# State recurrence of a two-layer block: four states in flight, SBUF operations over 1024 columns, and one accumulating transfer a state

## The chip, the cores and the metric

The kernel runs on one core of a Trainium2 chip. The metric is the device time of one execution in microseconds. Three runs of the kernel before gave 6723.36, 6741.94 and 6750.02 us; their median, 6741.94 us, is the time that the change is compared with.

## What is computed

The input is 16 sequences of 512 tokens with 256 features, in float32. Each sequence goes through two layers. Layer 0 is an attention whose scores are squared (q times k over 16 features a head, 16 heads, squared and made causal, then divided by their sum) and a gated product with int8 weights. Layer 1 is a state recurrence in both directions and a gated product whose operands are rounded to fp4 in blocks of 16. The recurrence sets the shape of the kernel. Per direction, with 512 channels `d` and 16 states `n`:

```python
dt = softplus(einsum('blr,dr->bld', dtr, Wdt) + bdt)
A  = -exp(Alog)
def step(h, ins):
    dt_t, u_t, B_t, C_t = ins
    h = exp(dt_t[..., None] * A) * h + (dt_t * u_t)[..., None] * B_t[:, None, :]
    y_t = einsum('bdn,bn->bd', h, C_t)
    return (h, y_t)
```

So for each of 32 pairs of direction and state the kernel scans 512 channels over 512 tokens and adds C times the result to a running sum y.

## The kernel before

**Slots.** Each engine runs a program of 128 slots per sequence (`SLOTS`), one slot for each group of 128 channels (`m`, four of them) of each of the 32 states. `one(b)` of each engine walks the slots. In each slot it issues its share of the recurrence and then its list of side work (`side`, L432) from a table, `PLAN`, that the `row(...)` calls from L284 on write out by hand: piece, direction, how many sequences ahead, and for each engine the slots of its items; a fraction orders items inside a slot. Five queues work through their own lists in order and meet only through semaphores. Side work of up to four neighbouring sequences lies in the slots of one: attention of sequence b+1, fp4 product of b-1, and so on. `sequences` (L441) runs b from -2 to 16, so that b = -2 and -1 fill the pipeline and the last ones drain it.

**The recurrence, by engine.** POOL multiplies B and dt*u into a state buffer (`inflow`, L723), three slots ahead of the scan. ScalarE (ACT) writes exp(dt*A) into one of three PSUM banks (`decay`, L943), two slots ahead. VectorE (DVE) scans in place (`scan`, L1214). When the four groups of a state are scanned, TensorE (PE) turns them, one block of 128 tokens per slot, into one of two PSUM banks (`turn_state`, L1497), four slots behind. Of the four token blocks of a state, DVE weighs two with C and adds them to `yT` in one operation (`add_state`, L1225). ACT weighs the other two into `hc` (`weigh_last`, L951), and POOL adds `hc` to `yT` (`add_last`, L734). Three state buffers `hb` (`HBS`) limit how far POOL can run ahead: `inflow` of state s waits until state s-3 has been turned.

**Side work of note.** Attention: `score` (L1307) makes products over 64 partitions, one head at a time; ACT squares them (`square`, L815), POOL masks them (`causal_mask`, L669), `weigh` (L1322) multiplies by v in column groups of 32 and `attn_divide` (L1081) ends a group of four heads. One of the three PSUM side banks (`SUMS`) is kept for the sums of `weigh` through slots 14 to 52 (`HELD`). The softplus of the step sizes takes four ACT operations, two DVE operations (L1178, L1180) and three POOL operations (L704, L707, L709) per group. `quantise` and `quantise_tail` round to fp4.

**Setup.** Before the slots, PE turns all weights, DVE rounds the fp4 weights (L991 to L1008), ACT and DVE evict the turned blocks, and SP stores them to DRAM; every engine waits until all 13 stores have landed. SP reloads weights into shared buffers later, in slots of the `l_` rows. SP also broadcasts one row of B per state into one of two halves of `bS` (`spread_b`, L636).

## Time and profile before

| | before |
|---|---|
| median of 3 runs | 6741.94 us |
| profiled execution, its own time | 6731.3 us |
| its span, first to last instruction | 6729.6 us |
| PE busy | 5027.9 us (75%) |
| POOL busy | 4928.8 us (73%) |
| DVE busy | 4791.3 us (71%) |
| ACT busy | 4129.1 us (61%) |
| granted TensorE clock, mean | 0.829 |

The profile is of one execution. Busy time is the time in which an engine has an instruction running; "idle before" is the time in which it had none just before the named instruction, with what ended the wait. The transfers took 14.4% of the time of the 16 DMA engines.

### The profile page before, as it was taken

What the parts mean: (1) busy time and instruction counts of PE and PEld (TensorE: products, weight loads), DVE (VectorE), ACT (ScalarE), POOL (GpSimd) and SP (SyncE); (2) the same over time, 40 slices, a digit from 0 to 9 for tenths busy, and PEclk for the clock granted to TensorE, in tenths of its full rate; (3) what the DMA queues carried; (4) which work ended last, traced back from release to release, by engine and by line L of the source; (5) the groups of instructions that cost most, each with busy time, mean ns of one, the idle gap of its engine ahead of it and who ended that gap; (6) DMA issues with size and microseconds to landing.
All of it is one profiled execution on the core that took longest, in us unless ns stands there. A gap on an engine that the chain in (4) does not pass through costs nothing.

```text
span 6729.6 us, 82733 instructions
## 1 busy us (share of the span) xinstructions
PE 5027.9 (75%) x21900; PEld 3136.3 (47%) x21900; DVE 4791.3 (71%) x6116; ACT 4129.1 (61%) x6696; POOL 4928.8 (73%) x3914
## 2 busy tenths in 40 slices
PE   3787777778778777877768777777877777787666
PEld 2344444454445444454444545444444544545444
DVE  3157777676877778687676867767687776868774
ACT  1366666666666666666666666666666666666563
POOL 0077777777777877778777777878777777777785
PEclk6678888888888888888888888888888888888777
DMA  3011111111111111111111111111111111111110
GB/s 111 15 43 38 51 45 47 38 47 45 50 51 47 45 42 45 46 51 50 40 50 40 50 45 48 45 38 53 40 50 51 47 47 38 45 46 48 37 46 26
DMA packets 152792, 308.76 MB, mean 46 GB/s; under 512 B 20870, under 2 KB 58310, under 8 KB 149926
## 3 DMA queue, kind: packets, MB, share of 16 engines
q1 hardware_dynamic: 152278, 302.80, 14.4%
q8 instruction: 214, 3.51, 0.2%
q14 instruction: 300, 2.46, 0.1%
HBM read 285.90 MB, written 16.84 MB: 45 GB/s over the span
## 4 chain that ended last, share of the span: by engine, by line
PE 47%; DVE 17%; issue 13%; POOL 11%; ACT 10%; DMA 1%; DVEq 0%; SPq 0%; POOLq 0%; ACTq 0%
PE psum L1497 8%; PE psum L1307 8%; POOL arena_m L723 5%; DVE arena_m L1214 4%; PE psum L1351 4%; PE psum L1422 3%; PE psum L1477 3%; PE psum L1430 3%; DVE arena_m L1164 3%; POOL arena_m L734 3%; PE psum L1385 3%; PE psum L1367 2%; PE psum L1439 2%; DVE arena_m L1225 2%; PE psum L1413 2%
## 5 line engine op out<-in xcount | busy, mean ns | idle before, releaser
L723 POOL TENSOR_TENSOR arena_m<-bS,arena_m 128x512 f32<-128x512 f32 x2048 | 2621.8, 1297 | 305.6 <-PE psum L1497 231.3
L1214 DVE TENSOR_TENSOR_SCAN arena_m<-psum,arena_m 128x512 f32<-128x512 f32 x2048 | 2448.0, 1209 | 322.4 <-POOL arena_m L723 193.6
L1497 PE MATMUL psum<-ident,arena_m 128*128 128x128 f32 x8192 | 1437.2, 312 | 540.1 <-DVE arena_m L1225 289.2
L734 POOL TENSOR_TENSOR arena_m<-arena_m,hc 128x512 f32<-128x512 f32 x1024 | 1307.3, 1277 | 569.0 <-ACT hc L951 345.7
L943 ACT ACTIVATE psum<-arena_m,Aneg 128x512 f32<-128x512 f32 x2048 | 1396.1, 690 | 428.2 <-DVE arena_m L1214 382.9
L1497 PEld LDWEIGHTS psum<-ident,arena_m 128*128 128x128 f32 x8192 | 1103.8, 160 | 1180.5 <-issue 535.6
L1225 DVE SCALAR_TENSOR_TENSOR arena_m<-psum,Ct,arena_m 128x512 f32<-128x512 f32 x1024 | 747.3, 730 | 379.8 <-PE psum L1497 375.0
L1307 PE MATMUL psum<-arena_a 64*128 64x512 f32 (+3 forms) x2048 | 829.2, 528 | 205.3 <-ACT arena_a L815 79.4
L951 ACT ACTIVATE hc<-psum,Ct 128x512 f32<-128x512 f32 x1024 | 696.3, 680 | 375.3 <-PE psum L1497 300.7
L815 ACT ACTIVATE arena_a<-psum 128x384 f32<-128x384 f32 (+1 forms) x768 | 401.8, 525 | 452.9 <-PE psum L1307 425.5
L1307 PEld LDWEIGHTS psum<-arena_a 64*128 64x128 f32 x2048 | 369.6, 208 | 541.3 <-issue 231.9
L1385 PE MATMUL psum<-wB,arena_m 128*128 128x352 f32 x1024 | 430.3, 553 | 84.2 <-DVE arena_m L1164 46.9
L669 POOL TENSOR_SCALAR_AFFINE_SELECT arena_a<-arena_a 128x512 f32<-128x512 f32 (+1 forms) x192 | 157.9, 822 | 394.4 <-ACT arena_a L815 394.3
L1164 DVE SCALAR_TENSOR_TENSOR arena_m<-psum,convw,arena_m 128x509 f32<-128x509 f32 (+2 forms) x384 | 286.7, 747 | 142.3 <-ACT arena_m L876 132.9
L1351 PE MATMUL psum<-arena_a,wA 128*128 128x512 bf16 x1152 | 323.2, 433 | 81.9 <-issue 55.4
L1422 PE MATMUL psum<-xnT,wU 128*128 128x512 f32 x512 | 289.7, 695 | 44.4 <-DVE arena_m L1164 43.5
L678 POOL TENSOR_TENSOR arena_a<-arena_a 128x704 f32<-128x704 f32 (+1 forms) x80 | 145.0, 1813 | 216.8 <-DVE arena_a L1002 216.8
L1385 PEld LDWEIGHTS psum<-wB,arena_m 128*128 128x128 f32 x1024 | 216.6, 234 | 178.2 <-issue 88.4
L1404 PE MATMUL psum<-ident,arena_a 128*128 128x128 f32 (+1 forms) x384 | 86.7, 360 | 275.9 <-POOL arena_a L684 217.4
L1430 PE MATMUL psum<-xnT,wZ 128*128 128x512 f32 x512 | 261.3, 642 | 0.5 <-ACT arena_m L918 0.5
L704 POOL TENSOR_TENSOR arena_m<-arena_m 128x512 f32<-128x512 f32 x128 | 170.7, 1333 | 104.4 <-ACT arena_m L903 104.3
L1477 PE MATMUL psum<-wO,arena_m 128*128 128x256 f32 x1024 | 237.2, 383 | 1.9 <-issue 0.8
(151 smaller groups left out, 7216.9 us busy)
## 6 DMA issues: line engine op xcount, KB each, us to landing
bS<-brow SPq DMA_DIRECT2D x512, 256.0 KB, 3.2
wB<-kept_B SPq DMA_DIRECT2D x16, 1408.0 KB, 6.2
wU<-kept_U SPq DMA_DIRECT2D x32, 512.0 KB, 4.5
wZ<-kept_Z SPq DMA_DIRECT2D x32, 512.0 KB, 4.6
wO<-kept_O SPq DMA_DIRECT2D x32, 512.0 KB, 4.8
wA<-kept_A SPq DMA_DIRECT2D x16, 768.0 KB, 5.6
wB<-kept_B SPq DMA_DIRECT2D x16, 768.0 KB, 4.3
wA<-kept_A SPq DMA_DIRECT2D x16, 640.0 KB, 4.2
```

The costliest lines, as they stand in the source:

```text
L723: pool.tensor_tensor(hb[s % HBS][:, m, :], bS[:, s % 2, :], du[r][:, m, :], ALU.mult).then_inc(m_dbu.sem, 1)
L734: pool.tensor_tensor(yT[:, 2 + i, :], yT[:, 2 + i, :], hc[:, i, :], ALU.add).then_inc(m_yl.sem, 1)
L943: act.activation(EB[j % EBS], dt[r][:, m, :], ACT.Exp, scale=Aneg[:, r, m, n:n + 1]).then_inc(m_dA.sem, 1)
L951: act.activation(hc[:, i, :], HT[1], ACT.Copy, scale=Ct[:, r, 2 + i, n:n + 1]).then_inc(m_hc.sem, 1)
L1164: dve.scalar_tensor_tensor(u[:, m, late:T], src[:, 0:T - late], convw[:, r, m, tap:tap + 1], u[:, m, late:T], ALU.mult, ALU.add).then_inc( ...
L1214: dve.tensor_tensor_scan(v, EB[j % EBS], v, 0.0, ALU.mult, ALU.add).then_inc(m_scan.sem, 1)
L1225: dve.scalar_tensor_tensor(yT[:, i, :], HT[0], Ct[:, r, i, n:n + 1], yT[:, i, :], ALU.mult, ALU.add).then_inc(m_y.sem, 1)
L1307: ins = pe.matmul(bank("a_score", None, w)[:, c:c + n], kT[rows, ht, i * P:(i + 1) * P], qm[rows, j, i * P:T], start=True, stop=True)
L1351: ins = pe.matmul(bank(piece, None, m), w[:, k, m * P:(m + 1) * P], xparts[:, c, k, :], start=(k == 0 and c == 0), stop=(k == KD - 1 and c ...
L1385: ins = pe.matmul(bank(piece, None, w)[:, 0:FIH], xTq[:, k, i * P:(i + 1) * P], w_[:, k, c * FIH:(c + 1) * FIH], start=(k == 0), stop=(k = ...
L1422: ins = pe.matmul(bank("p_in", r, m), wU[:, k, m * P:(m + 1) * P], xnT[:, k, :], start=(k == 0), stop=(k == KD - 1))
L1497: ins = pe.transpose(HT[pos % 2][:, m * P:(m + 1) * P], hb[s % HBS][:, m, i * P:(i + 1) * P], ident[:, :])
```

## The change

The change has six parts.

1. Recurrence. There are four state buffers in place of three (`HBS`). `inflow` becomes one POOL operation on 128x1024 for two channel groups, every second slot, four slots ahead. `turn_state` runs six slots behind the scan in place of four (`TURN`). It turns the token blocks in the order 0, 1, 2, 3; DVE adds blocks 0 and 1, ACT weighs blocks 2 and 3.
2. `add_last` is no POOL operation any more but one DMA transfer per state, issued by POOL: `hc` (now 4 KB a partition for each of two states) is added to `yT[:, 2:4, :]`, 512 KB. It waits for both blocks of `hc` and for the transfer of the state before.
3. Attention. `score` issues the products of two heads, one on partitions 0 to 63 and one on 64 to 127, in turn. `weigh` runs once per group of four heads and takes any free side bank, which is held until the division. `asq` is laid out in four parts; `square` has one more operation for every third item, the mask is 16 operations of 128x512, and the division is two operations.
4. Softplus. The correction takes one DVE operation in place of two and one more ACT operation.
5. Setup. The fp4 weights are not rounded before the slots but in slots 12 to 17 of b = -1, turned in slots 36 to 49, stored from slot 56; the waits for the stores move to slot 92 of b = -1, SP's wait for the first ten stays in slot 0 of it.
6. Space and plan. `wZ` shares its buffer with `wU`, `wX` with `wO`; their loads wait for each other's readers. All rows of `PLAN` are new.

The diff, cut to its core:

```diff
-    HBS = 3
+    HBS = 4
-    ORDER = (0, 2, 1, 3)
+    TURN = 6
-        wZ = sb("wZ", [P, KD, DI])
-        wX = sb("wX", [P, NM, P])
+        wZ = wU
+        wX = wO[:, 0:NM // 2, :].rearrange("p m (h c) -> p (m h) c", h=D // P)
-        hc = sb("hc", [P, 2, DI])
+        hc = sb("hc", [P, 2, 2, DI])
...
-        row("d_turn", 1, -1, PE=[4, 4.2, 4.3, 6.1])
+        row("d_turn", 1, -1, PE=[3, 3, 7, 7])
...
-        row("p_in", 1, 0, PE=[13, 16, 19.1, 22], ACT=[14, 16, 19, 22])
+        row("p_in", 1, 0, PE=[14, 16, 18, 21], ACT=[14, 17, 19, 22])
...
+        row("l_X", 1, 0, SP=[8])
+        row("d_out", 1, -1, PE=[9, 10, 11, 11.1], DVE=[10, 12])
...
+        FRONT, FP4_IN, FP4_DVE, FP4_PE, FP4_OUT, FREE = 0, 2, 12, 36, 56, 92
...
@@ gpsimd @@
                 if m == 0:
-                    before = s - HBS if s >= HBS else min(s - 2, -1)
-                    pool.wait_ge(*m_hT.by(b, NT * (before + 1)))
+                    pool.wait_ge(*m_hT.by(b, NT * (s - HBS + 1)))
...
-                pool.tensor_tensor(hb[s % HBS][:, m, :], bS[:, s % 2, :], du[r][:, m, :], ALU.mult).then_inc(m_dbu.sem, 1)
+                two = slice(m, m + 2)
+                pool.tensor_tensor(hb[s % HBS][:, two, :], bS[:, s % 2, :].unsqueeze(1).to_broadcast([P, 2, T]), du[r][:, two, :],
+                                   ALU.mult).then_inc(m_dbu.sem, 1)
...
+            def add_last(b, s):
                 r, n = divmod(s, NS)
-                pool.wait_ge(*m_hc.by(b, c + 1))
+                pool.wait_ge(*m_hc.by(b, 2 * s + 2))
                 if n == 0:
-                    pool.wait_ge(*m_y0.by(b, NT * r + 2 + i + 1))
+                    pool.wait_ge(*m_y0.by(b, NT * (r + 1)))
                 else:
-                    pool.wait_ge(*m_yl.by(b, c - 1))
-                pool.tensor_tensor(yT[:, 2 + i, :], yT[:, 2 + i, :], hc[:, i, :], ALU.add).then_inc(m_yl.sem, 1)
+                    pool.wait_ge(*m_yl.by(b, 16 * s))
+                apart(pool)
+                pool.dma_start(yT[:, 2:4, :], hc[:, s % 2, :, :], accum_op=ALU.add).then_inc(m_yl.sem, 16)
...
-                    ab, ja = spot(b, j + 3)
-                    if exists(ab):
+                    ab, ja = spot(b, j + 4)
+                    if ja % 2 == 0 and exists(ab):
                         inflow(ab, ja)
-                    if j % 2:
-                        lb, jl = spot(b, j - 7)
-                        if exists(lb):
-                            add_last(lb, jl // 2)
+                    lb, jl = spot(b, j - TURN - 3)
+                    if jl % NT == NT - 1 and exists(lb):
+                        add_last(lb, jl // NT)
...
@@ scalar @@
-                act.activation(src, src, ACT.Exp, scale=-1.0).then_inc(m_ex.sem, 1)
+                act.activation(cx[:, c, :], src, ACT.Exp, scale=-1.0).then_inc(m_ex.sem, 1)
...
-                act.activation(lx[:, c, :], src, ACT.Ln, bias=1.0).then_inc(m_ln.sem, 1)
+                act.activation(src, cx[:, c, :], ACT.Identity, bias=1.0).then_inc(m_w.sem, 1)
+                act.wait_ge(*m_w.by(b, q + 1))
+                act.activation(lx[:, c, :], src, ACT.Ln).then_inc(m_ln.sem, 1)
...
-                act.wait_ge(*m_yl.by(b, c - 1))
-                act.activation(hc[:, i, :], HT[1], ACT.Copy, scale=Ct[:, r, 2 + i, n:n + 1]).then_inc(m_hc.sem, 1)
+                act.wait_ge(*m_yl.by(b, 16 * (s - 1)))
+                act.activation(hc[:, s % 2, i, :], HT[i], ACT.Copy, scale=Ct[:, r, 2 + i, n:n + 1]).then_inc(m_hc.sem, 1)
...
+                    wb, jw = spot(b, j - TURN - 2)
+                    if jw % NT >= 2 and exists(wb):
+                        weigh_last(wb, 2 * (jw // NT) + jw % NT - 2)
...
@@ vector @@
-                dve.tensor_scalar(cx[:, c, :], src, 1.0, -1.0, ALU.add, ALU.add).then_inc(m_c1.sem, 1)
-                dve.wait_ge(*m_c1.by(b, q + 1))
-                dve.tensor_tensor(cx[:, c, :], src, cx[:, c, :], ALU.subtract).then_inc(m_c2.sem, 1)
+                dve.scalar_tensor_tensor(cx[:, c, :], bank("p_dt", r, m), 1.0, cx[:, c, :], ALU.subtract,
+                                         ALU.subtract).then_inc(m_c2.sem, 1)
...
+                    if first(b) and FP4_DVE <= j < FP4_DVE + 6:
+                        fp4_weights(j - FP4_DVE)
...
+                    yb, jy = spot(b, j - TURN - 1)
+                    if jy % NT < 2 and exists(yb):
+                        add_state(yb, 2 * (jy // NT) + jy % NT)
...
@@ tensor @@
+                if w % 2 == 0:
+                    apart(pe)
+                    return
                 for i, c in UNITS[un]:
                     n = T - i * P
-                    ins = pe.matmul(bank("a_score", None, w)[:, c:c + n], kT[rows, ht, i * P:(i + 1) * P], qm[rows, j, i * P:T],
-                                    start=True, stop=True)
-                ins.then_inc(a_s_ps.sem, 1)
+                    for half in range(2):
+                        rows = slice(64 * half, 64 * half + 64)
+                        ins = pe.matmul(bank("a_score", None, w - 1 + half)[:, c:c + n], kT[rows, ht, i * P:(i + 1) * P],
+                                        qm[rows, j, i * P:T], start=True, stop=True)
...
-                    pe.wait_ge(*m_yl.by(b, 2 * (NS * (r + 1) - 1) + i - 1))
+                    pe.wait_ge(*m_yl.by(b, 16 * NS * (r + 1)))
...
-                if pos % 2 == 0:
-                    pe.wait_ge(*m_y.by(b, c // 2))
+                if i < 2:
+                    pe.wait_ge(*m_hc.by(b, 2 * s - 1 + i))
                 else:
-                    pe.wait_ge(*m_hc.by(b, c // 2))
+                    pe.wait_ge(*m_y.by(b, 2 * s - 1 + i))
```

## Rows read from the trace of the kernel before

**Rows 1.** The page, busy time by engine and its slices.

```profile
PE 5027.9 (75%) x21900; PEld 3136.3 (47%) x21900; DVE 4791.3 (71%) x6116; ACT 4129.1 (61%) x6696; POOL 4928.8 (73%) x3914
```

**Rows 2.** All scans (L1214): duration, first and last start, who waits.

```profile
L1214 DVE TENSOR_TENSOR_SCAN arena_m<-psum,arena_m x2048: 1158/1211/1226, 367.8 to 6619.8; 128x512 f32<-128x512 f32 x187
```

**Rows 3.** One sequence by stage: stretch, busy (x instructions) of PE, PEld, DVE, ACT, POOL, clock, DMA.

```profile
3117.00:3138.00 21.00, 14.60 (x80) 12.54 (x81) 14.33 (x16) 9.50 (x15) 18.47 (x16) 0.76 0.22 64
3138.00:3262.00 124.00, 107.20 (x454) 55.22 (x451) 83.53 (x102) 81.00 (x142) 91.15 (x78) 0.88 0.13 39
3262.00:3302.00 40.00, 26.43 (x136) 17.52 (x136) 32.65 (x43) 28.24 (x46) 38.11 (x32) 0.78 0.17 51
3302.00:3400.00 98.00, 77.10 (x377) 54.17 (x378) 79.88 (x105) 63.99 (x97) 69.79 (x51) 0.90 0.17 55
3400.00:3516.00 116.00, 81.09 (x322) 51.80 (x321) 85.94 (x114) 73.93 (x120) 92.08 (x71) 0.84 0.14 41
```

**Rows 4.** Groups of POOL, same sequence: count, busy us, mean ns, idle before it.

```profile
L723 POOL TENSOR_TENSOR arena_m<-bS,arena_m 128x512 f32<-128x512 f32 x129 | 165.3, 1299 | 19.8 <-PE psum L1497 14.6 <-DMA bS<-brow 5.2
L734 POOL TENSOR_TENSOR arena_m<-arena_m,hc 128x512 f32<-128x512 f32 x65 | 83.0, 1277 | 35.5 <-ACT hc L951 21.3 <-ACT arena_m L913 13.9
...
L697 POOL TENSOR_TENSOR xL<-xA,arena_a 128x1024 f32<-128x1024 f32 x1 | 2.4, 2350 | 4.7 <-ACT arena_a L782 4.7
```

**Rows 5.** DMA issues by line: KB each, median us from issue to landing.

```profile
bS<-brow SPq DMA_DIRECT2D x512, 256.0 KB, 3.2
wB<-kept_B SPq DMA_DIRECT2D x16, 1408.0 KB, 6.2
wU<-kept_U SPq DMA_DIRECT2D x32, 512.0 KB, 4.5
...
wO<-kept_O SPq DMA_DIRECT2D x32, 512.0 KB, 4.8
...
out<-xF SPq DMA_DIRECT2D x16, 512.0 KB, 3.0
```

**Rows 6.** Products of score (L1307) and weigh (L1322), same sequence, columns of rows 3.

```profile
3117.00:3516.00 399.00, 50.00 (x128) 22.09 (x128) 0.85 0.15 46
...
3117.00:3516.00 399.00, 11.10 (x128) 2.98 (x128) 0.85 0.15 46
```

**Rows 7.** PE in order of time: start, us; weigh in four column groups, then score.

```profile
3213.48 0.86 PE L1322 MATMUL psum<-arena_a,vx 128*32 128x256 f32 x16
...
3216.92 0.91 PE L1307 MATMUL psum<-arena_a 64*128 64x384 f32 x2
```

**Rows 8.** Groups of DVE and of ACT, same sequence.

```profile
L1178 DVE TENSOR_SCALAR arena_m<-psum 128x512 f32<-128x512 f32 x8 | 5.5, 682 | 9.2 <-ACT arena_m L903 9.2
...
L903 ACT ACTIVATE arena_m<-psum 128x512 f32<-128x512 f32 x8 | 4.8, 598 | 0.6
```

**Rows 9.** Setup in order of time: Aneg on ACT, first fp4 step, PE resumes, PE in slots.

```profile
36.29 0.31 ACT L753 ACTIVATE Aneg<-arena_m 128x128 f32<-128x128 f32 x1 [34.19 <-DMA arena_m<-in_L_attn_b_Alog]
...
31.82 1.22 DVE L991 TENSOR_REDUCE hc<-arena_m 88x64 f32<-88x1024 f32 x1 [8.11 <-DMA arena_m<-in_L_ffn_w_down]
...
79.63 4.89 PE L1252 MATMUL psum<-ident,arena_m 128*128 128x128 f32 x28 [59.84 <-DVE arena_m L1030]
...
122.65 1.94 PE L1263 MATMUL psum<-ident,arena_a 128*128 128x128 f32 x8 [30.46 <-ACT arena_a L782]
```

**Rows 10.** Two stretches of the fill, columns of rows 3.

```profile
122.00:250.00 128.00, 112.94 (x336) 54.95 (x336) 7.96 (x25) 38.35 (x73) 9.84 (x12) 0.59 0.03 10
250.00:366.00 116.00, 70.40 (x208) 35.94 (x209) 35.56 (x73) 47.54 (x73) 29.25 (x23) 0.76 0.12 34
```

**Rows 11.** Waits in the same sequence: total us, times, longest.

```profile
DVE arena_m L1225 <- PE psum L1497: 23.0, 10, 4.8
POOL arena_m L734 <- ACT hc L951: 21.3, 9, 6.2
...
POOL arena_m L734 <- ACT arena_m L913: 13.9, 2, 8.8
```

More of the change, by code:

```diff
@@ new lines, in block_kernel @@
+        row("f_rest", None, 1, DVE=[63, 64, 66, 66])
+        row("f_gate", None, 1, PE=[65, 65, 67, 67, 68.2, 70], ACT=[68, 68, 69, 69, 70.1, 72.1])
+        row("q_quant", None, -1, DVE=[66, 67, 67, 69, 70, 71], POOL=[78, 78, 80])
+        row("d_turn", 0, 0, PE=[68, 68.1, 73, 74])
+        row("i_turn", 1, 0, PE=[69, 71, 75.1, 75.2], ACT=[70, 72, 77, 78])
+        row("f_silu", None, 1, ACT=[69, 74])
+        row("d_gate", 0, 0, DVE=[69, 69, 74, 74.2])
+        row("f_up", None, 1, PE=[71, 72, 74, 75, 76, 77.1], DVE=[73, 74.1, 75, 76, 77, 78])
@@ new lines, in block_kernel @@
+        row("d_out", 0, 0, PE=[77, 78, 80, 80], DVE=[78, 83])
+        row("f_down", None, 1, PE=[78, 80, 82, 82], DVE=[81, 84])
+        row("z_in", 1, 0, PE=[81, 84, 86, 86], ACT=[82, 86.1, 86.2, 89])
+        row("m_stat2", None, 1, ACT=[86], DVE=[81, 85, 85])
+        row("q_turn", None, -1, PE=[83, 83], ACT=[84, 85])
+        row("m_norm2", None, 1, ACT=[88], DVE=[86])
+        row("m_x", None, 1, POOL=[88])
+        row("q_gate", None, -1, PE=[89, 90, 94, 96, 101.1, 102, 106.1, 108], ACT=[90, 91, 95.1, 97.1, 103, 103, 108, 108])
@@ L390, in block_kernel @@
         }
-        HELD = range(14, 53)
+        divided = [j for j in range(SLOTS) for q in PLAN["DVE"][j] if q[0] == "a_sums"]
+        held = {}
         jobs_of = [[], [], []]
@@ L1030, in _, with fp4_weights @@
                 dve.tensor_copy(dst, src).then_inc(setup_dve.sem, 1)
-            dve.wait_ge(setup_act.sem, NJ // 2)
-            dve.wait_ge(a_neg.sem, 2)
-            dve.wait_ge(stored.sem, 16 * (STORES + 1))
+            for n in range(0, NJ, 2):
+                evict(n)
+            def fp4_weights(part):
+                s, c = divmod(part, 2)
+                rows, cols = (GP, 8 * D) if s < 2 else (P, KD * FI)
+                half = cols // 2
+                dve.wait_ge(loaded["fp4"].sem, 16 * 3)
+                if part:
+                    dve.wait_ge(wquant.sem, QOPS * part)
+                for k in range(QOPS):
+                    quantise(s_fp4[s][0:rows, c * half:(c + 1) * half], wtmp[0:rows, 0:half], w_am, w_sc, w_inv, 0, wquant,
+                             QOPS * part, k)
             def norm_stat(n, b, src, k):
```

430 lines of the change are left out of this document (220 added, 210 removed).

## The prediction

> **What bounds the kernel now.** I read the page first. No engine is full: PE 75%, POOL 73%, DVE 71%, ACT 61% of the span [rows 1]. So the limit is not one engine but the five in-order queues that follow one another within a few slots; in each stage the busiest one sets the pace and the others wait for it.
>
> The second view is the line of the scans, one per slot. There are 2048 from 367.8 to 6619.8 us [rows 2], 6252 us; over 2047 intervals that is 3.054 us a slot, 391 us a sequence; with full side work it is 399 us, as in the sequence of [rows 3]. Before the first scan lie 368 us of setup and fill, behind the last 109 us of drain. The first sequences lack some side work, so I take 397 us for a full one and count the stretch as 6252 / 397 = 15.75 sequences.
>
> The third view cuts one sequence into five stages [rows 3]. The reader is to see that the bound moves:
> - 3117 to 3138 (slots 0 to 7, the change of direction): POOL 18.5 of 21 us.
> - 3138 to 3262 (8 to 47, attention): PE 107.2 of 124 us, 86%; POOL 91.2, DVE 83.5, ACT 81.0.
> - 3262 to 3302 (48 to 63): POOL 38.1 of 40 us, 95%; DVE 32.7.
> - 3302 to 3400 (64 to 95): DVE 79.9 and PE 77.1 of 98 us; nobody is full.
> - 3400 to 3516 (96 to 127, fp4 and the next softplus): POOL 92.1 of 116, DVE 85.9, PE 81.1.
>
> The fourth view, the waits, shows the lockstep: in this sequence DVE's add waits 23.0 us for turned blocks, and POOL's add 21.3 us for ACT's `hc` and 13.9 us for the first terms [rows 11].
>
> **The change part by part.** Against the profiled execution (6731.3 us), per sequence unless said otherwise.
>
> (a) POOL loses 64 adds of 1277 ns, 82 us [rows 4]. A pair of inflows costs 2 x 1299 = 2.60 us now; one operation on 128x1024 took 2.35 us [rows 4], so 64 of them save 0.25 x 64 = 16 us. It gains 32 DMA issues. No row shows POOL issuing a DMA. I bound one issue by nothing (all beside other work) and by the two adds that it replaces, 2.55 us, and take 1.3 us, one POOL operation on 512 columns: 42 us. The net is about -56 us, between -98 and -16.
>
> (b) The transfer. 512 KB were stored in 3.0 us and loaded in 4.5 and 4.8 us; 1408 KB took 6.2 us [rows 5], so 896 KB more cost 1.7 us. An accumulate must also read its destination. Counted as 1024 KB it lands in 4.5 + 512 / 896 x 1.7 = 5.5 us. The ends are 3.0 us and two full loads, 9.6 us. POOL waits for the transfer of the state before, in its queue, and behind that wait stand the next inflow, the softplus sums and fp4 tails; DVE's scan waits for the inflow. So the distance of two issues, 5.5 + 1.3 = 6.8 us, is a floor for a state. A state takes 12.2 us in the mean (four slots), but not evenly. Of the 511 distances from each fourth scan of [rows 2] to the next, 104 are under 8 us. With every distance shortened by 7%, the floor adds about 60 us in the run at 6.8 us, 181 us at 8 us and 435 us at 10 us. I take 60 us.
>
> By the Trainium skill, page DMA: Bandwidth & Descriptors, section Anatomy of one DMA, a transfer issued by GpSimd takes about 2.0 us and its bytes over 436 GB/s. As an estimate from that page, with 1 MB, that is 4.4 us and the 60 us would be near 5. No row here shows a transfer of this kind.
>
> At each change of direction PE's `d_turn` of blocks 2 and 3 waits for the last transfer; it is issued in POOL's slot 8, while `d_turn` stands in PE's slot 7. Before, it waited for one 1.3 us add. That is up to 5.5 us, twice a sequence, in stages where PE works 14.6 of 21 us. I charge the first stage its whole gain (3 us) and nothing more.
>
> (c) Attention. The scores hold PE for 50.0 us in 128 instructions [rows 6]. They use 64 partitions. The trace has no pair on both halves, but it has the other split: 16 weigh products in four column groups took 0.86 us, less than two score products of 384 columns, 0.91 us [rows 7]. So groups do overlap on this PE, and I take half, -22 us (ends 0 and -25). What is late next in the attention stage: PE 85, DVE 83.5 less 32 corrections and a few, 81, ACT 81 + 4 us (part d), POOL 91 less 25. At 80% for the busiest, the stage takes 85 / 0.8 = 106 us in place of 124: 18 us. All three side banks serve the scores between the holds, which works the same way; I don't count it apart.
>
> By the Trainium skill, page TensorEngine Tiling (Array Packing), section PSUM Bottleneck, tiling speeds up PE but not the evacuation of PSUM. If that ruled here, ACT's squares would be late next and the 18 us would shrink to nearly nothing, which is the second rival's result.
>
> (d) Softplus: DVE loses 8 x 682 ns = 5.5 us, ACT gains one operation like L903, 8 x 598 ns = 4.8 us [rows 8], and 16 short squares. ACT is the least busy of the four, so I cost its part at nothing; without that cover it is 9 us.
>
> (e) The other stages. Slots 48 to 63: POOL falls from 38.1 to about 28, DVE at 32.7 in 0.9 of the time gives 36 us: 4 us. Slots 64 to 95: no bound is removed, but the turn has three slots of room behind the scan in place of one, and the inflow four in place of three: 3 us. Slots 96 to 127: POOL falls from 92 to about 77, and DVE's 86 at 79% give 109 us: 6 us, as POOL's three-operation softplus chain stays. Slots 0 to 7: nothing. The sum is 18 + 4 + 3 + 6 = 31 us; I take 3 off for SP, whose queue now stands at `l_X` in slot 8 until PE's `d_out` of slot 11, with the next B rows behind it. 28 us a sequence, 28 x 15.75 = 441 us.
>
> (f) Setup. The fp4 rounding starts at 31.8 us and PE resumes at 79.6 us behind it [rows 9]: 48 us. Then come the stores and their landing, and PE turns the first attention block at 122.7 us [rows 9]. Without the rounding ACT's evictions still wait for `Aneg`, 36.3 us [rows 9]; 13 of them by 0.6 us end at 44, and with some 7 us for the first norm the same turn comes at about 54 us. That is 68 us. The rounding moves beside the fill's attention, where DVE works 8.0 of 128 us while PE works 112.9 [rows 10]; it is hidden but for the divisions behind it, and without this cover it costs its 48 us. I charge 15 us for it and the 18 moved turns. The score pairs take about 20 us off the same stage. The drain gets two slots longer and a transfer, 6 us. Net -67 us.
>
> **The sum.** 6731.3 - 441 + 60 - 67 = 6283 us in the profiled execution. The median of the runs is 10.6 us above that execution's time, so the median after is 6294, rounded to 6290 us.
>
> **The rivals.**
>
> 1. The accumulating transfer is the bound (slower). It is one chain of 512 transfers, each waiting for the one before. Its price is set by the distance L of two issues. With all other gains, the run takes 6681 us at L = 10, 6876 at 11, 7121 at 12 and 7444 at 13; it decides from L = 10.3 us. For it: no transfer inside SBUF, issued by POOL or adding is in the trace, and 10.3 is only 0.7 above my upper end of 9.6 plus no issue time. Against it: 512 KB land in 3.0 to 4.8 us [rows 5] and the DMA engines are used to 0.14 to 0.22 [rows 3]. Its time: 7120 us.
>
> 2. The score pairs don't overlap, or ACT's squares take PE's place. Then the attention stage gives 2 in place of 18 us: 16 x 15.75 = 252 us dearer, 6540 us. For it: ACT works 81 of 124 us there, and scores wait for banks. Against it: the column groups overlap [rows 7].
>
> 3. The lockstep stays. PE's turn of block 0 now waits in the slot in which ACT weighs block 2 of the state before, where there was a slot between them; what the longer distances give is lost there. POOL's gain is hidden, only setup counts: 6742 - 67 + 30 = 6705 us. For it: no engine was above 86% over 124 us. Against it: two stages have an engine at 86 and 95%.
>
> 4. Looser queues give more. With the busiest engine at 90% in the middle stages a sequence takes 340 us: 57 x 15.75 = 898 us off, 5840 us with (b) and (f). For it: there are more buffers in every loop but the two PSUM banks. Against it: DVE reaches such shares only in stretches.
>
> **How the numbers follow.** Forecast 0.48 (6120 to 6450, most of it from the landing time); rival 2 0.15; rival 3 0.12; rival 4 0.08; rival 1 0.17. Half a per cent (34 us) is about what a measurement tells from no change. Rival 3 lies on that edge; a bit over half of it counts as the same: same 0.07. Faster 0.48 + 0.15 + 0.05 + 0.08 = 0.76. Slower 0.17. The range, 5990 to 6750 us, leaves out half of rival 4 and rival 1 nearly whole, 0.2.
>
> **What would show each step.** POOL busy near 4000 us, with a gap or an issue of 1 to 2 us at each transfer; landings of 5 to 6 us in the list of DMA issues. The score line at 25 to 30 us a sequence. The scans' stretch at 5870 us, the first one at about 300 us. In the stages, PE and DVE near 80% in slots 8 to 47. I am wrong on the sign if POOL's longest wait in total is for its own transfers and states come at equal distances; wrong on (c) if two score products in a pair start one after another.

## The result and the profile after

The changed kernel takes 6798.6 us (6791.6 to 6807.8), the kernel before in the same runs 6743.3 us (6723.4 to 6750.0): ratio 1.0088, 95% interval 1.0063 to 1.0113. It is slower by 0.9%, where 6290 us was predicted, with a range of 5990 to 6750 us. The mean granted TensorE clock is 0.828, against 0.829 before, so the clock is not what differs.

Every piece of work that was to go did go. The page of the changed kernel: busy time by engine, the DMA queue of POOL (packets, MB, share of the 16 DMA engines), groups of instructions (busy us, mean ns, idle before) and the issue of the transfer with its landing in us; beside [rows 1], [rows 4] and [rows 5]:

```profile
span 6793.3 us, 80279 instructions
PE 4619.7 (68%) x21853; PEld 2952.4 (43%) x21900; DVE 4730.9 (70%) x6052; ACT 4209.5 (62%) x7080; POOL 3926.6 (58%) x2442
...
q0 software_dynamic: 73728, 268.47, 21.1%
...
L762 POOL TENSOR_TENSOR arena_m<-bS,arena_m 128x1024 f32<-128x1024 f32 x1024 | 2547.7, 2537 | 983.0 <-PE psum L1565 509.7
...
L774 POOL DMA_DIRECT2D arena_m<-hc x512 | 468.5, 915 | 684.6 <-ACT hc L999 491.0
...
L1378 PE MATMUL psum<-arena_a 64*128 64x512 f32 (+3 forms) x2048 | 443.4, 535 | 160.6 <-ACT arena_a L860 66.8
...
arena_m<-hc POOLq DMA_DIRECT2D x512, 512.0 KB, 4.6
```

POOL has 1002 us less work, PE 408 us, the transfer is issued in 0.9 us, has landed after 4.6 us and takes up 21% of the DMA engines. And yet the scans, with the first and last start beside [rows 2], take longer:

```profile
L1268 DVE TENSOR_TENSOR_SCAN arena_m<-psum,arena_m x2048: 1157/1214/1225, 289.8 to 6669.0; 128x512 f32<-128x512 f32 x187
```

The first scan comes 78 us earlier, the stretch from first to last is 6379 us in place of 6252, the drain 124 in place of 110. So all of the loss lies in the stretch from the first scan to the last. One sequence by stage, in the columns of [rows 3] and cut at the same slots (0 to 7, 8 to 47, 48 to 63, 64 to 95, 96 to 127):

```profile
3094.00:3107.00 13.00, 8.83 (x48) 7.41 (x48) 12.43 (x14) 8.33 (x14) 9.58 (x6) 0.71 0.45 93
3107.00:3247.00 140.00, 91.30 (x475) 51.03 (x476) 88.37 (x105) 84.34 (x160) 71.37 (x52) 0.85 0.31 72
3247.00:3288.00 41.00, 26.84 (x159) 18.69 (x157) 29.30 (x44) 30.23 (x50) 30.86 (x20) 0.82 0.41 96
3288.00:3387.00 99.00, 72.11 (x352) 49.58 (x356) 77.95 (x105) 62.45 (x95) 54.14 (x29) 0.87 0.43 110
3387.00:3498.00 111.00, 82.99 (x327) 53.58 (x326) 81.68 (x110) 76.66 (x124) 79.35 (x49) 0.84 0.34 81
```

The attention stage, where PE was to fall from 107 to 85 us and the stage from 124 to 106, has PE at 91 and lasts 140 us: its busiest engine is at 65%. (Most of that loss lies in the first eight of these slots; see the table below.) The stage of slots 48 to 63 lost 7 us of POOL's work and takes 41 us where it took 40. What is there instead are waits. The list of the changed kernel (total us, times, longest):

```profile
DVE arena_m L1279 <- PE psum L1565: 791.4, 415, 8.7
PE psum L1565 <- ACT hc L999: 748.7, 448, 7.3
...
POOL arena_m L762 <- PE psum L1565: 509.7, 151, 9.6
...
POOL arena_m L774 <- ACT hc L999: 491.0, 125, 12.0
POOL arena_m L762 <- DMA bS<-brow: 473.1, 61, 18.4
...
PE psum L1537 <- DMA arena_m<-hc: 79.4, 16, 9.3
```

The same list for the queue of SP alone:

```profile
SPq L658 <- ACT xd L936: 945.1, 31, 48.0
SPq L589 <- PE psum L1546: 832.9, 30, 33.0
...
SPq L646 <- POOL xL L736: 264.0, 15, 53.4
```

The same waits of the kernel before, in the same columns: PE's turn for ACT's `hc`, and POOL's inflow for the broadcast B rows.

```profile
PE psum L1497 <- ACT hc L951: 122.0, 121, 4.6
...
POOL arena_m L723 <- DMA bS<-brow: 74.3, 15, 5.8
```

Three suspects stand in these lists: PE's turn waits for ACT's weighing (the new order 0, 1, 2, 3), POOL waits for B rows that SP fetches (the SP queue stands at `keep_rows`, L658, and at `l_X`, L589), and `d_turn` (L1537) waits for the transfer. A list of waits doesn't say what a wait costs, so each was tried in a kernel of its own.

### The profile page after: what moved, and what is told of

Read it like the earlier page. It is cut to its first block and busy times, and to the rows that moved or that the text cites. A ratio compares the mean times of both kernels' runs of the same rounds, so it can differ in the third digit from the quotient of the medians.

```text
span 6793.3 us, 80279 instructions
## 1 busy us (share of the span) xinstructions
PE 4619.7 (68%) x21853; PEld 2952.4 (43%) x21900; DVE 4730.9 (70%) x6052; ACT 4209.5 (62%) x7080; POOL 3926.6 (58%) x2442
## 3 DMA queue, kind: packets, MB, share of 16 engines
q1 hardware_dynamic: 152278, 302.80, 14.1%
## 5 line engine op out<-in xcount | busy, mean ns | idle before, releaser
L762 POOL TENSOR_TENSOR arena_m<-bS,arena_m 128x1024 f32<-128x1024 f32 x1024 | 2547.7, 2537 | 983.0 <-PE psum L1565 509.7
L1268 DVE TENSOR_TENSOR_SCAN arena_m<-psum,arena_m 128x512 f32<-128x512 f32 x2048 | 2443.1, 1210 | 201.5 <-ACT psum L991 167.8
L774 POOL DMA_DIRECT2D arena_m<-hc x512 | 468.5, 915 | 684.6 <-ACT hc L999 491.0
L860 ACT ACTIVATE arena_a<-psum 128x512 f32<-128x512 f32 (+3 forms) x1024 | 381.4, 444 | 523.6 <-PE psum L1378 342.1
L708 POOL TENSOR_SCALAR_AFFINE_SELECT arena_a<-arena_a 128x512 f32<-128x512 f32 x256 | 193.8, 814 | 669.1 <-ACT arena_a L860 668.9
L1378 PE MATMUL psum<-arena_a 64*128 64x512 f32 (+3 forms) x2048 | 443.4, 535 | 160.6 <-ACT arena_a L860 66.8
L1454 PE MATMUL psum<-wB,arena_a 128*128 128x352 f32 x1024 | 412.1, 541 | 62.2 <-DVE arena_m L1222 60.3
L1328 PE MATMUL psum<-ident,arena_a 128*128 128x128 f32 x640 | 128.9, 361 | 331.4 <-ACT arena_a L825 282.2
L1378 PEld LDWEIGHTS psum<-arena_a 64*128 64x128 f32 x2048 | 195.1, 216 | 312.6 <-issue 178.0
L1491 PE MATMUL psum<-xnT,wU 128*128 128x512 f32 x512 | 267.5, 649 | 32.2 <-DVE arena_m L1222 29.7
L1454 PEld LDWEIGHTS psum<-wB,arena_a 128*128 128x128 f32 x1024 | 210.4, 223 | 162.0 <-issue 55.1
L1499 PE MATMUL psum<-xnT,wU 128*128 128x512 f32 x512 | 257.1, 638 | 4.5 <-DVE xA L1172 4.2
```

Of the source, the lines that this page charges most:

```text
L762: pool.tensor_tensor(hb[s % HBS][:, two, :], bS[:, s % 2, :].unsqueeze(1).to_broadcast([P, 2, T]), du[r][:, two, :], ALU.mult).then_inc(m_ ...
L774: pool.dma_start(yT[:, 2:4, :], hc[:, s % 2, :, :], accum_op=ALU.add).then_inc(m_yl.sem, 16)
L860: act.activation(asq[i][:, 2 * (j % 2) + j // 2, :], bank("a_score", None, w)[:, c:c + n], ACT.Square).then_inc(a_sq.sem, 1)
L1268: dve.tensor_tensor_scan(v, EB[j % EBS], v, 0.0, ALU.mult, ALU.add).then_inc(m_scan.sem, 1)
L1378: ins = pe.matmul(bank("a_score", None, w - 1 + half)[:, c:c + n], kT[rows, ht, i * P:(i + 1) * P], qm[rows, j, i * P:T], start=True, stop ...
L1454: ins = pe.matmul(bank(piece, None, w)[:, 0:FIH], xTq[:, k, i * P:(i + 1) * P], w_[:, k, c * FIH:(c + 1) * FIH], start=(k == 0), stop=(k = ...
```

## The experiments

b-kernels edit the kernel before, e-kernels the changed one. Where a kernel also needs small moves of side work, its expectation says so. Kernels are compared by their medians; the 95% intervals of the ratios are about 0.2% (some 12 us) to either side. The table is worked out from the starts of the scans (mean over sequences 3 to 14 of the 16, us for each range of slots; the column in brackets is a part of the one before it) and is used throughout:

```
kernel        first scan  sequence   0-7   8-31  (8-15)  32-47  48-63  64-95  96-127
before            367.8     397.9   21.3   63.8  (13.5)   59.3   40.1   99.3   114.2
after             289.8     406.2   13.6   76.5  (27.6)   63.4   40.8  101.1   110.8
b1_dma            368.8     408.8   27.8   65.1  (13.4)   61.0   39.4  104.4   111.1
b2_order          350.9     447.7   28.0   82.3  (16.2)   68.7   42.6  106.4   119.7
e2_sp_rows        295.1     397.3   13.5   76.4  (27.7)   58.6   39.2   99.0   110.5
e3_pool_add       293.8     407.6   13.6   74.7  (25.2)   60.0   44.3  102.4   112.6
e1_alternate      296.3     402.5   13.9   77.9  (32.1)   59.1   42.0  102.7   106.9
e5_alt_sp         297.9     392.2   14.0   78.6  (32.5)   51.2   42.8   99.0   106.7
e10_change        296.2     388.0   14.0   72.2  (27.4)   54.4   41.5   98.9   106.9
e14 (one half)    306.8     420.3   13.5   87.8  (31.2)   66.5   40.0  101.6   110.8
```

The table shows where the changed kernel loses its 8.3 us a sequence. Slots 0 to 7 get 7.7 us shorter and slots 8 to 15 get 14.1 us longer: with the turn six slots behind the scan, the end of the direction before (`d_turn`, gate, `d_out`) stands in later slots, partly behind slot 7. Slots 0 to 15 together go from 34.8 to 41.2 us. Slots 16 to 47, the rest of the attention, take 112.3 us where they took 109.6, although PE's work there fell from 93.6 to 70.3 us.

**The transfer alone, and the order alone, in the kernel before.**

b1_dma:

```diff
-                pool.tensor_tensor(yT[:, 2 + i, :], yT[:, 2 + i, :], hc[:, i, :], ALU.add).then_inc(m_yl.sem, 1)
+                pool.dma_start(yT[:, 2:4, :], hc[:, s % 2, :, :], accum_op=ALU.add).then_inc(m_yl.sem, 16)
```

> The kernel before with the accumulating transfer alone: one transfer a state in place of two POOL additions, hc for two states, space made by letting the fp4 product's input share a buffer with the attention's; order, distances and side work as before. Theory C: slower than before, 6800 us or more. Theories A and B: faster, by 1 to 4%, 6470 to 6680 us, since POOL's 1307 us of additions become 470 us of issues and nothing else is touched.

Measured: 6857.6 us, ratio 1.019 (1.0173 to 1.0208). The transfer makes the kernel before slower by 122 us, as theory C had it. (The shared buffer of the fp4 input, which makes the space, was not tried apart.) Its page and its waits:

```profile
PE 5041.7 (74%) x21838; PEld 3158.7 (46%) x21900; DVE 4818.1 (70%) x6116; ACT 4123.4 (60%) x6696; POOL 4068.0 (59%) x3402
...
L723 POOL TENSOR_TENSOR arena_m<-bS,arena_m 128x512 f32<-128x512 f32 x2048 | 2723.5, 1488 | 960.7 <-PE psum L1497 795.9
```

```profile
PE psum L1468 <- DMA arena_m<-hc: 129.8, 17, 8.7
```

POOL lost 861 us and waits 796 us for PE's turns in their place (231 before). In slots 48 to 63, where POOL had been 95% busy [rows 3], its work fell from 38.0 to 30.3 us and the stage only from 40.1 to 39.4 us: POOL's work alone did not set it. 6.5 of the 10.9 us lost a sequence lie in slots 0 to 7, where `d_turn` now waits for a landing.

b2_order puts the new turning order into the kernel before at its distance of four slots:

```diff
-                i = ORDER[pos]
-                if pos % 2 == 0:
-                    pe.wait_ge(*m_y.by(b, c // 2))
+                if i < 2:
+                    pe.wait_ge(*m_hc.by(b, 2 * s - 1 + i))
```

> The kernel before with one part of the change alone: token blocks turned in the order 0, 1, 2, 3, DVE adding the first two and ACT weighing the last two, all distances and side work as before. Theory A (the order costs the time: PE's turn now waits for ACT's weighing in the same slot, 748.7 us in the changed kernel against 122.0): slower than before by 2 to 6%, about 6880 to 7150 us, with PE's wait for the hc line at 30 us a sequence or more. Theory B (SP's queue stands at its own waits and the B rows come late) and theory C (the accumulating transfer costs it): within 0.7% of before, 6700 to 6790 us.

Measured: 7447.0 us, ratio 1.1056 (1.1038 to 1.1075), the largest effect of all the runs: theory A in kind, but far above its 2 to 6%.

```profile
DVE arena_m L1222 <- PE psum L1492: 868.8, 461, 6.3
PE psum L1492 <- ACT hc L949: 843.3, 489, 5.6
```

The turn of block 0 and ACT's weighing of block 2 of the state before now stand in one slot and wait for one another in turn; DVE's add stands behind. It costs in every range of slots, most in the attention.

**What the order costs at greater distances.** `TURN` is the distance of the turn behind the scan, six in the changed kernel.

e7_turn5 sets `TURN = 5` in the changed kernel. e6_alt5 sets it too and restores the old order (its core):

```diff
-    TURN = 6
+    TURN = 5
+    ORDER = (0, 2, 1, 3)
```

> Control for the one before: the changed kernel with the turn five slots behind the scan, in the changed kernel's own order. Both theories: 6750 to 6900 us; if it is faster than 6700 us, the distance and not the order explains a gain of the one before.

> The changed kernel with the old order of the token blocks (0, 2, 1, 3; DVE and ACT take turns, one PSUM bank each) and the turn five slots behind the scan in place of six; every row of side work as in the changed kernel. Theory A (the order is what eats the gain): 6200 to 6550 us, and PE's wait for the hc line falls from 748.7 us below 250 us. Rival (the long wait for hc is only PE's slack, since PE is 68% busy here): within 1% of the changed kernel, 6730 to 6870 us.

Measured: e7_turn5 7136.6 us (ratio 1.0605), e6_alt5 6761.1 us (1.0046). Both times miss what was expected. e7_turn5 lies above its range: the sixth slot alone is worth 338 us in the new order. e6_alt5 lies in the rival's range, although PE's wait for `hc` fell to 219 us as theory A had it; only beside e7_turn5 does it show that at distance five the order costs 376 us.

e1_alternate has the old order at distance six; `d_turn` of the first direction, one pair of scores and one softplus row are moved by a slot.

> The changed kernel (6799 us) with the turning order of before, 0, 2, 1, 3, at its own distance of six slots: PE's turn and ACT's weighing of one state lie in different slots again. A first-stage d_turn, one pair of scores and one softplus row are shifted by one slot, since at this order and distance the queues would otherwise wait in a circle. It computes the same. Theory (the order is a cost that the distance of six hides only in part): at a distance of five the order was worth 7137 - 6761 = 376 us, so here some of it remains; PE's wait for ACT's hc falls from 749 to under 300 us in total and the time lies at 6600 to 6720 us. Rival (at six slots the order costs nothing more, what is left comes from the SP queue and the side plan): 6780 to 6820 us, with the wait gone but the same time lost elsewhere.

Measured: 6717.2 us (6703.1 to 6727.5), ratio 0.9977 (0.9968 to 0.9987), 1.2% under the changed kernel.

```profile
POOL arena_m L763 <- PE psum L1567: 720.5, 139, 13.8
...
POOL arena_m L763 <- DMA bS<-brow: 460.0, 61, 21.7
...
PE psum L1567 <- ACT hc L1000: 347.1, 164, 6.6
```

The wait for `hc` fell by 402 us and the time by only 81; POOL's wait for the turns grew from 510 to 721 us in its place. So the order costs 712 us at distance four, 376 at five, 81 at six. The first of these is from the kernel before, which differs in more than the distance, and the last includes the moved side work: slots 8 to 15 got 4.5 us longer here, slots 16 to 47 7.4 us shorter. The time lies at the upper end of the theory's range, but the wait didn't fall under 300.

**The SP queue.** e2_sp_rows moves six rows of the changed kernel's SP plan behind what they wait for:

```diff
-        row("p_rows", 1, 0, SP=[26])
-        row("l_X", 1, 0, SP=[8])
-        row("l_X", 0, 1, SP=[78])
-        row("l_x", None, 2, SP=[86])
+        row("p_rows", 1, 0, SP=[42])
+        row("l_X", 1, 0, SP=[12])
+        row("l_X", 0, 1, SP=[86])
+        row("l_x", None, 2, SP=[92])
```

(and `l_g1` from 82 to 84, `store` from 119 to 122).

> The changed kernel with six rows of SP's list moved to later slots, behind what they wait for (p_rows from 26 to 42, l_X from 8 to 12 and from 78 to 86, l_g1 82 to 84, l_x 86 to 92, store 119 to 122). Theory B: POOL's wait for the B rows (473 us) falls below 120 us and with it the time, to 6400 to 6550 us. Theory A: that wait falls, but PE's and DVE's waits grow in its place; 6700 to 6800 us. Theory C: no change, 6750 to 6800 us.

Measured: 6648.1 us (6647.6 to 6651.0), ratio 0.9874 (0.9857 to 0.989), 2.2% under the changed kernel and already faster than before. The wait for the B rows fell below 120 us as theory B had it; the time stayed above its 6400 to 6550 us. Its waits:

```profile
PE psum L1565 <- ACT hc L999: 799.0, 438, 7.4
...
POOL arena_m L762 <- DMA bS<-brow: 105.8, 15, 7.4
```

```profile
SPq L658 <- ACT xd L936: 267.1, 16, 32.6
```

`keep_rows` had been moved by the change from slot 42 to 26, while ACT writes `xd` in slot 32 of its plan; `l_X` had gone from 14 to 8 and `l_x` from 102 to 86. SP stood there, the B rows behind it were not fetched, POOL's inflow stood without them, and DVE's scan without the inflow. With the row back at 42, slots 32 to 47 fall from 63.4 to 58.6 us; 1.6 us more come in slots 48 to 63 and 2.1 in 64 to 95. The six rows were moved together, so what each is worth is read only from where the slots got shorter. The wait for `hc` grew in the same run by 50 us, and the time fell all the same.

**The two causes together, and the change of direction.** e5_alt_sp has the old order at distance six and the SP rows moved:

> The kernel of the run before this one (order 0, 2, 1, 3, distance six) with the six rows of the SP queue moved as in e2_sp_rows. It computes the same. Theory (order and SP queue are two separate costs): 150 us below e1_alternate, and below e2_sp_rows (6648 us) by what e1_alternate lies below the changed kernel, so 6450 to 6600 us. Rival (both were ways of waiting for one bound that lies under both, such as DVE's and POOL's own work in the stages): 6620 to 6670 us, the same as e2_sp_rows.

Measured: 6555.7 us (6552.6 to 6561.9), ratio 0.9741 (0.9724 to 0.9757). The order gives 92 us here and 81 without the SP rows, the SP rows 161 and 151: at distance six these are two costs that add up. e8_alt5_sp, the same at distance five:

> Old order, turn five slots behind, and the six rows of SP's list behind what they wait for. If the two causes are separate, the time falls by the gain of the old order and by the 150 us of SP's rows: 6050 to 6400 us. If they share the same stall, it is that of the old order alone.

Measured: 6678.1 us, ratio 0.9931, far above the expected 6050 to 6400. At distance five the SP rows are worth only 83 us (6761.1 against 6678.1), so the two costs don't add up there. The sixth slot is worth 122 us, and 44 without the SP rows moved.

In both the changed kernel and e5_alt_sp one place stands out. The changed kernel in order of time at the first change of direction, first PE, then DVE (start, us, in brackets the idle time before and its releaser):

```profile
3106.14 0.63 PE L1565 MATMUL psum<-ident,arena_m 128*128 128x128 f32 x4
3111.28 1.96 PE L1537 MATMUL psum<-ident,arena_m 128*128 128x128 f32 x8 [4.51 <-DMA arena_m<-hc]
...
3117.81 1.89 PE L1546 MATMUL psum<-wO,arena_m 128*128 128x256 f32 x8
```

```profile
3113.89 1.21 DVE L1268 TENSOR_TENSOR_SCAN arena_m<-psum,arena_m 128x512 f32<-128x512 f32 x1
3122.00 0.69 DVE L1251 TENSOR_TENSOR xF<-psum,xM 128x512 f32<-128x512 f32 x1 [6.89 <-PE psum L1546]
3122.61 1.21 DVE L1268 TENSOR_TENSOR_SCAN arena_m<-psum,arena_m 128x512 f32<-128x512 f32 x1
```

`d_turn` stands in PE's slot 7, the transfer that it needs is issued in POOL's slot 8. PE idles 4.5 us, and then turn, gate and `d_out` follow in a chain while no scan runs: 8.7 us between two scans. e10_change moves the chain behind the transfer:

```diff
-        row("d_turn", 1, -1, PE=[3, 5, 7, 7])
-        row("d_gate", 1, -1, DVE=[6, 6, 9, 9])
-        row("d_out", 1, -1, PE=[9, 10, 11, 11.1], DVE=[10, 12])
-        row("l_X", 1, 0, SP=[12])
+        row("d_turn", 1, -1, PE=[3, 5, 9, 9])
+        row("d_gate", 1, -1, DVE=[6, 6, 10, 10])
+        row("d_out", 1, -1, PE=[11, 11, 12, 12.1], DVE=[12, 13])
+        row("l_X", 1, 0, SP=[15])
```

> e5_alt_sp (6556 us) with the turn of blocks 2 and 3 at the first change of direction moved from PE's slot 7 to slot 9, behind the transfer that it waits for, the gate that follows from DVE's slot 9 to 10, the first d_out from 9 and 10 to 11, and one row of the SP queue (l_X) from 12 to 15, as it waits for d_out. It computes the same. In e5_alt_sp the scans of slots 9 and 10 take 18.7 us of the 388.6 us of a sequence: PE stands 4.1 us for the transfer, then turn, gate, d_out and correction follow one another with the other engines idle (DVE 9.4 us for d_out, POOL 22 us for the squares behind it). Theory (the period is made of such waits of a queue's head; with the turn behind the transfer they go): slots 8 to 15 fall from 32.5 to under 27 us, the run by 60 to 120 us, 6440 to 6500 us. Rival (the chain only moves, two slots later): 6540 to 6570 us.

Measured: 6485.0 us (6480.9 to 6497.1), ratio 0.9644 (0.9626 to 0.9662), 71 us under e5_alt_sp. Slots 8 to 31 fall by 6.4 us; slots 8 to 15 alone from 32.5 to 27.4, a little short of the theory. Slots 32 to 47 give 3.2 us of it back, so that a sequence is 4.2 us shorter. Slots 0 to 15 still take 41.4 us, where the kernel before took 34.8.

**What the transfer is worth.** e3_pool_add puts one POOL add of 128x1024 a state in the place of the transfer, in the changed kernel; e11_alt_sp_add does so in e5_alt_sp.

```diff
-                pool.dma_start(yT[:, 2:4, :], hc[:, s % 2, :, :], accum_op=ALU.add).then_inc(m_yl.sem, 16)
+                pool.tensor_tensor(yT[:, 2:4, :], yT[:, 2:4, :], hc[:, s % 2, :, :], ALU.add).then_inc(m_yl.sem, 1)
```

> The changed kernel with the transfer replaced by one POOL operation on 128x1024 a state. Theory C: faster than the changed kernel, 6500 to 6700 us, since waits for the transfer and its landing go. Theories A and B: the same as the changed kernel or slower by up to 3%, 6790 to 7000 us, since POOL's busy time rises by about 512 x (2.5 - 0.9) = 820 us, to 4750 us.

> e5_alt_sp (6556 us) with one POOL add of 128x1024 a state in place of the accumulating transfer. It computes the same. It measures what the transfer is worth once the order and the SP queue no longer hold the queues up. Theory (POOL's busy time is not what sets the pace, the transfer frees it for little and costs its landing at the change of direction): within 0.7% of 6556 us, 6530 to 6600. Rival (the freed POOL time counts as soon as the other waits are gone, as the prediction had it, some 10 us a sequence): 6680 us or more.

Measured: e3_pool_add 6832.2 us (ratio 1.0151), 0.5% above the changed kernel; e11_alt_sp_add 6704.4 us (0.9972), 149 us above e5_alt_sp. So the third suspect costs the changed kernel nothing on the whole: without the transfer it gets slower and not faster, and theory C fell there. In the table e3_pool_add is shorter by 5.2 us in slots 0 to 47 and longer by 3.5 us in slots 48 to 63: there POOL's work does count in this kernel, which b1_dma did not show in the kernel before. The theory behind e11_alt_sp_add fell too: POOL's 0.75 ms are worth 34 us while other waits hold the queues and 149 us when these are gone.

**What the overlapping scores are worth.** Three runs were to take the overlap out and didn't: e4_unpaired (in the changed kernel), e9_sp_unpaired (in e2_sp_rows), e12_unpaired (in e10_change).

```diff
-                    for half in range(2):
-                        rows = slice(64 * half, 64 * half + 64)
+                rows = slice(64 * (w % 2), 64 * (w % 2) + 64)
```

> The changed kernel with each head's score product issued by itself, no pair on the two partition halves. My forecast gave the pair 16 us a sequence: 6980 to 7080 us. Rival (in this kernel PE is not what sets the attention stage, so the 386 us of PE time that went are slack): 6790 to 6880 us. In both the score line's busy time goes back from 443 to about 830 us.

> e2_sp_rows (6648 us) with the scores computed one product after another, as before, in place of pairs on both halves of PE; PE works some 385 us more. It computes the same. Theory (the scores lie off the path, whatever the SP queue does): 6640 to 6680 us. Rival (the 386 us were hidden only because the SP queue's rows set the period of a sequence): with those rows moved the pairs count, at the size of the prediction's 18 us a sequence in part, so 6750 to 6900 us.

> e10_change (6485 us) with the scores one product after another in place of pairs; PE works some 385 us more. It computes the same. It asks of the pairs what e11_alt_sp_add asked of the transfer, whose worth grew from 0.5% in the changed kernel to 2.3% with order and SP queue mended. Theory (what an operation saves counts only where no queue waits for another): the pairs' worth grows as well, from 9 us in the changed kernel and 40 us in e2_sp_rows to 60 to 150 us, 6545 to 6635 us. Rival (the scores stay beside other work): 6480 to 6530 us.

Measured: 6807.6 us (ratio 1.0116), 6688.5 us (0.9939) and 6468.8 us (0.9614, interval 0.9598 to 0.963). The expectations of some 385 us more work for PE are wrong, and with them what their theories were to show. The score line of e4_unpaired:

```profile
L1374 PE MATMUL psum<-arena_a 64*128 64x512 f32 (+3 forms) x2048 | 541.8, 529 | 104.9 <-DVE arena_m L1222 36.0
```

542 us, not 829: successive heads lie on different halves of the rows, so their products overlap whether or not one function writes them in pairs. What these runs measure is the interleaving alone: +9, +40 and -16 us without it, of which only the 40 are well clear; in the other two the intervals overlap. The lowest time of all is that of e12_unpaired, 3.9% under the kernel before.

To take the overlap away all products have to lie on one half. The two kernels below do that, in the changed kernel and in e10_change; the edit is shown against e4_unpaired and e12_unpaired, which they have to be compared with.

```diff
-                rows = slice(64 * (w % 2), 64 * (w % 2) + 64)
+                rows = slice(0, 64)
```

> The changed kernel (6799 us) with the scores one product after another and all of them on the lower half of PE's rows, so that no two can overlap. The odd heads get the products of the even ones: that part of the output is not the reference's, the amount of work is the same. It is needed because e4_unpaired, e9_sp_unpaired and e12_unpaired did not do what their expectations said: there the score line still took 542 us against 443, since successive products lay on different halves and went on overlapping. Expected: the score line at 800 to 850 us, PE some 350 to 390 us busier. Theory (in the changed kernel the scores lie beside the waits of order and SP queue): 6800 to 6860 us. Rival (PE sets the attention stage, the prediction's step): 284 us dearer, 7050 us or more.

> The same edit on e10_change (6485 us): all scores on the lower half of PE's rows, no overlap, the odd heads' scores being those of the even ones. Expected: the score line at 800 to 850 us. Theory (as with the transfer, the saving counts once the queues are mended): 6550 to 6650 us. Rival 1 (scores never counted): 6470 to 6510 us, as e12_unpaired. Rival 2 (the prediction's 18 us a sequence were right in size and only covered): 6740 us or more.

Measured: e14_after_one_half 6989.7 us, ratio 1.0379 (1.0358 to 1.0399); e13_one_half 6610.4 us, ratio 0.9818 (0.9801 to 0.9834). The page of e14_after_one_half:

```profile
PE 5071.0 (73%) x21900; PEld 3219.7 (46%) x21900; DVE 4731.9 (68%) x6052; ACT 4228.4 (60%) x7080; POOL 3926.5 (56%) x2442
...
L1374 PE MATMUL psum<-arena_a 64*128 64x512 f32 (+3 forms) x2048 | 851.2, 554 | 83.6 <-DVE arena_m L1222 36.0
```

The theory that the scores lie beside other waits fell too, and the rival's 7050 us was not reached; e13_one_half lies in its theory's range. The overlap is worth 182 us in the changed kernel (6989.7 against 6807.6; 191 against the changed kernel itself) and 142 us in the fastest version, so unlike the transfer it is not worth more there. Against the changed kernel, slots 8 to 47 get 14.4 us longer (139.9 to 154.3 a sequence) and the first scan comes 17 us later. Of PE's 451 us more in e14_after_one_half, 408 lie in the score line; the mean granted clock is 0.810 in place of 0.828, and the turns (L1560) take 1469 us in place of 1440. What the clock adds to the price was not separated.

## Why the prediction was wrong, step by step

- **(a), (b) POOL and the transfer.** POOL's total was right (near 4000 us; 3927), in part by luck: the issues cost 0.9 in place of 1.3 us each, some 200 us less, and the wider inflows saved some 200 us less than charged (last section). The landing, 5 to 6 us, was 4.6. The estimate of 4.4 us from the Trainium skill, page DMA: Bandwidth & Descriptors, section Anatomy of one DMA, was nearer to the 4.6 us than the 5.5 of the rows. POOL waits only 16.7 us in the whole run for its own transfer, so the 60 us for the floor were too much, and rival 1 was not near. (Its prices are also 12 us above the prediction's own terms: 6283 - 60 + 435 + 10.6 gives 6669 us at L = 10, not 6681.) The sign came out wrong without the sign of it that was named, a longest wait of POOL for its own transfers. The change of direction was seen, and charged at 3 us a sequence, the whole gain of slots 0 to 7; the chain behind the wait was not followed, and moving it gave 4.2 us a sequence (388.0 against 392.2) for one of the two directions. Slots 0 to 15, where the sum has no loss, got 6.4 us longer. e3_pool_add, with no transfer, takes 38.8 of these 41.2 us, so 4.0 of the 6.4 us are not the landing; what makes them up was not tried by a run.
- **(c) The scores.** "I take half" was right: 829 to 443 us. So was nearly the price: 18 us a sequence predicted, 14.4 measured by taking the overlap out, and 17 us for the 20 in the fill. Rival 2 did not come: ACT still takes every product out of PSUM, and the overlap is worth 182 us. By the Trainium skill, page TensorEngine Tiling (Array Packing), section PSUM Bottleneck, the PSUM copy may become the bottleneck after a fourfold speedup of TensorE; here the score line was sped up 1.9 times, and these runs show no such limit.
- **The step that failed is the pace.** The prediction took, for each stage, the busiest engine and its share, and let the stage shrink with its work, "at 80% for the busiest". The stages did not follow it. In slots 16 to 47 PE, the busiest engine, lost 23.3 us of work and fell from 85% to 63%, and the stretch got 2.7 us longer. In b1_dma POOL's share in slots 48 to 63 was 95%, its work fell by 7.7 us, and the stage gave 0.7 us; in the whole change it gave none of the 4 that were charged. What the sum left out is the waits that the new order, the SP rows and the change of direction bring: the overlap of (c) is worth nearly what was charged, and slots 8 to 47, in which it lies, still take 139.9 us where they took 123.1. e2_sp_rows, e5_alt_sp and e10_change show it from the other side: they take no operation off any engine, they only order them otherwise, and the last is 314 us under the changed kernel.
- **(e) The SP queue.** "I take 3 off for SP" named `l_X` in slot 8 and left out `keep_rows`, which the change moves from slot 42 to 26, six slots ahead of ACT's `xd`. The SP rows cost 8.9 us a sequence (406.2 against 397.3), 151 us in the run, where 3 us a sequence were charged.
- **Rival 3, the lockstep.** Its mechanism, "PE's turn of block 0 now waits in the slot in which ACT weighs block 2 of the state before", is in the trace (122 to 749 us) and costs 81 us at distance six. It had no price of its own in the sum. The rival's time, 6705 us, had no SP queue in it; with the SP rows mended and the lockstep left, e2_sp_rows took 6648 us.
- **(f) Setup.** Net -67 predicted. The first scan came 78 us earlier, the drain took 15 us more in place of 6: -63. Right.
- **The sum of the parts stays open.** Order (81 us), SP rows (161 behind it) and the chain (71) are 314 us: taking them out one after another gives 6485 in place of 6799. The remaining 195 us to 6290 are not explained by a run. The table says where they lie. Against the kernel before, e10_change has 10.4 of the 18 us in slots 16 to 47 and 7.3 us for the 6 charged in slots 96 to 127; slots 48 to 95 got 1.0 us longer where 7 were charged, and slots 0 to 15 got 6.6 us longer. That POOL got slower (last section) may be a part of it. The moved side work of the other stages and the softplus of part (d) were not tried one by one.

## What to carry to other kernels

Before summing what a change saves on an engine, list every instruction that it moves past another in each in-order queue, the DMA-issuing queue too, and set each one's slot beside the slot of what it waits for: six rows of an SP plan cost 2.2%, and two queues that meet in one slot 1 to 11% by their distance. A busy share of 95% did not show a bound; the run that took work away did. What a saving is worth depends on the waits around it: the same transfer cost 122 us in the kernel before and was worth 34 and 149 us in two others. Set the stages side by side slot by slot as well: a chain that moves from one stage into the next looks like a loss of the second. An experiment that undoes a part must be read at its own line first: three of these left the overlap in place.

## What the runs showed of the hardware

A transfer of 512 KB that adds within SBUF was issued by POOL in 0.9 us and landed in 4.6 us, and while such transfers run POOL's own operations are slower. In the changed kernel's own trace, the 398 inflows (L762) that ran with no such transfer between issue and landing took 2356 ns in the mean, and the 411 that had one beside them for over 80% of their time 2677 ns; the masks (L708) took 643 and 1038 ns. DVE's scans took 1209 and 1210 ns. The inflows that had only SP's transfers of the B rows beside them took 2353 ns. POOL's inflow over the whole run, from the groups of instructions, in e11_alt_sp_add (without the transfer), then in e5_alt_sp (with it):

```profile
L763 POOL TENSOR_TENSOR arena_m<-bS,arena_m 128x1024 f32<-128x1024 f32 x1024 | 2414.9, 2369 | 600.0 <-PE psum L1566 550.1
```

```profile
L763 POOL TENSOR_TENSOR arena_m<-bS,arena_m 128x1024 f32<-128x1024 f32 x1024 | 2537.6, 2521 | 950.4 <-PE psum L1567 845.1
```

2369 against 2521 ns, 6% more; in b1_dma the 128x512 form went from 1297 ns (whole run; 1299 in the sequence of [rows 4]) to 1488, 15%. So the prediction's price for the wider inflow, 2.35 us, holds without the transfer (2369 ns, 14 us a sequence for the 16), and the transfer takes most of it: 2594 - 2537 = 57 ns each, 3.6 us a sequence.

Small operations of DVE are held up beside POOL's. In the changed kernel, the 21 of the 80 normalisation steps L1103 (128x4) that had no POOL operation beside them took 170 ns in the mean; the 44 that had one beside them for over 90% of their time took 2099 ns, and up to 9.8 us. DVE's busy time holds such stretches: it is 4519 us in e2_sp_rows and 4843 us in e1_alternate, with the same operations. What they cost the kernel was not tried.
